# Last pass of a graph network kernel: the rows of 104 of its 416 tiles fetched by one-hot matmuls, the other 312 gathered into places of their own

## The reference, cut to what matters

```
# L3: x_i = x[row], x_j = x[col]; row and col are the edges' two ends
m   = [x_i, x_j - x_i] @ W.T, batch norm, silu        # per edge
out = segment_sum(m, row)                              # one sum per node, added to x
```

## Time and profile before

| | |
|---|---|
| median of 3 runs | 4434.35 us (4432.85 to 4438.28) |
| the profiled execution's own time | 4435.5 us |
| its span | 4433.7 us |
| granted clock of TensorE, mean | 0.892 of 2.4 GHz |
| PE busy | 3310.6 us (75%) |
| DVE busy | 2910.4 us (66%) |
| POOL busy | 3018.6 us (68%) |
| the last pass, from its first gather to the end of the span | 3891.8 to 4433.7 us |

### The profile page before, as it was taken

One profiled execution on the slowest core, in us unless ns is written; L12 is line 12 of the kernel. 1 busy time (PEld: TensorE's weight loads), 2 busy tenths in 40 slices (PEclk: granted clock), 3 DMA queues, 4 the chain that ended last, 5 costly groups with the idle time before them and its releaser, 6 DMA issues.

```text
span 4433.7 us, 80945 instructions
## 1 busy us (share of the span) xinstructions
PE 3310.6 (75%) x20757; PEld 2267.7 (51%) x20758; DVE 2910.4 (66%) x10438; ACT 847.9 (19%) x2207; POOL 3018.6 (68%) x3059
## 2 busy tenths in 40 slices
PE   1269408888887999999687876888858877566666
PEld 1269304554553444443466665666646666445554
DVE  6987319999993111111788887888878888765554
ACT  0000002222221000000122222222212222121121
POOL 2677767788778888840377774777747777467776
PEclk9999999999997999999899996999979999755555
DMA  4310013333458999999222223222232222211112
GB/s 143 108 46 10 17 59 81 88 90 90 92 88 314 356 363 356 363 357 361 80 62 62 61 62 51 63 62 62 62 52 63 62 62 62 33 32 28 28 28 30
DMA packets 295276, 497.76 MB, mean 112 GB/s; under 512 B 165611, under 2 KB 210540, under 8 KB 293674
## 3 DMA queue, kind: packets, MB, share of 16 engines
q1 hardware_dynamic: 120119, 340.02, 21.7%
q0 software_dynamic: 92160, 115.39, 13.6%
q10 hardware_dynamic: 82800, 40.01, 3.1%
HBM read 435.66 MB, written 59.08 MB: 112 GB/s over the span
## 4 chain that ended last, share of the span: by engine, by line
PE 29%; POOL 24%; issue 18%; DMA 16%; DVE 9%; DVEq 1%; SPq 1%; ACT 1%; POOLq 0%; ACTq 0%
PE ps L1565 27%; POOL arena L825 17%; DMA arena<-table,arena 13%; POOL rows_dst L808 7%; DMA rows_dst<-stage,arena 2%; PE ps L1754 1%; DMA arena<-in_edge_attr_dram 1%; DVE arena L1174 1%; DVE arena L1173 1%; DVE arena L1156 1%; DVEq L553 1%; DVE arena L1158 1%; DVE arena L1192 1%; DVE arena L1150 1%; DMA arena<-dense 1%
## 5 line engine op out<-in xcount | busy, mean ns | idle before, releaser
L825 POOL DMA_INDIRECT arena<-table,arena x2080 | 2110.2, 1015 | 1046.5 <-issue 541.3
L1565 PE MATMUL ps<-arena 125*128 (+5 forms) x9976 | 1629.7, 339 | 580.5 <-DVE arena L1192 250.9
L1565 PEld LDWEIGHTS ps<-arena 125*128 125x128 bf16 (+5 forms) x9976 | 1187.8, 206 | 990.8 <-issue 606.5
L1565 PE MATMUL ps<-arena,nodes 125*64 125x500 f32 (+2 forms) x3144 | 651.4, 537 | 34.6 <-DMA arena<-dense 24.1
L1174 DVE TENSOR_SCALAR arena<-iota_row_b,arena 128x128 f32<-128x128 bf16 x2080 | 584.9, 299 | 0.0
L808 POOL DMA_INDIRECT rows_dst<-stage,arena x400 | 401.0, 1002 | 233.0 <-issue 122.2
L779 POOL DMA_INDIRECT rows_src<-stage,stage_at x400 | 479.0, 1197 | 116.4 <-issue 108.4
L1186 DVE TENSOR_TENSOR arena<-ps,arena 128x256 f32<-128x256 f32 x416 | 176.6, 425 | 523.9 <-DMA arena<-table,arena 510.4
L1173 DVE TENSOR_SCALAR arena<-iota_row_b,arena 128x128 bf16<-128x128 bf16 x1664 | 458.4, 277 | 2.7 <-DVE arena L1325 1.1
L1274 DVE TENSOR_TENSOR nodes<-nodes,ps 125x256 f32 (+1 forms) x70 | 27.5, 393 | 609.4 <-PE ps L1754 609.4
L1565 PEld LDWEIGHTS ps<-arena,nodes 125*64 125x64 f32 (+1 forms) x3144 | 244.5, 137 | 351.7 <-issue 320.1
(11 more groups left out here) (286 smaller groups left out, 3510.3 us busy)
## 6 DMA issues: line engine op xcount, KB each, us to landing
arena<-dense SPq DMA_DIRECT2D x240, 750.0 KB, 7.5
nodes<-dense SPq DMA_DIRECT2D x60, 750.0 KB, 8.2
dense<-arena ACTq DMA_DIRECT2D x150, 250.0 KB
arena<-table,arena POOLq DMA_INDIRECT x2080
arena<-dense SPq DMA_DIRECT2D x60, 500.0 KB
arena<-rows_dst SPq DMA_DIRECT2D x208, 96.0 KB
arena<-dense SPq DMA_DIRECT2D x6, 2000.0 KB, 21.5
arena<-pair_rows SPq DMA_DIRECT2D x12, 976.6 KB
```

The source lines that it names most:

```text
L825: nc.gpsimd.indirect_dma_start(rows[:, u, k, 0:width], None, frm, bass.IndirectOffsetOnAxis(ap=p[:, c, j, c_other:c_other + 1].bitcast(I32 ...
L1565: return nc.tensor.matmul(to, lhsT, rhs, start=start, stop=stop, skip_group_check=True)
```

## The change

Only the last pass's way to its rows is replaced; three things are prepared for it earlier. In the changed kernel:

1. With tables (`pair_...`): for each of the 25 blocks of other nodes and each block of own nodes it is known which tiles hold such edges (edges of one own block are sorted by the other's block). Going through the tiles in order, a step is one (tile, block of the other nodes) pair that occurs: at most 104 + 600 = 704 steps for the first 104 tiles. The tables are worked out behind those of before, ahead of `blk_ready`: some 60 DVE instructions, four transposes, a 25-wide product, 20 matmuls of 1 x 384, 30 of 128 x 2, one more, and 15 small DMAs in three round trips to DRAM.
2. In the second of the third layer's passes SP loads all 416 tiles' (key, other) into `src_rows` (852 KB), DVE makes a code for each edge (6 more instructions and a copy), PE turns codes and keys in 8 transposes ahead of its pass, ACT copies them, SP writes them to DRAM. In the third POOL issues 6 indirect DMAs more, DVE one subtraction, and SP writes `turn_rows`.
3. In the last pass SP loads keys, broadcast to all partitions, 256 KB for two units (`load_keys`). DVE makes the turned one-hots directly, 128 x 512 f32 from f16 keys (`turn_step`), with no transpose by PE and no copy by ACT. PE first goes through the 704 steps in 44 iterations of 16: each step is one f32 matmul, turned one-hot (128 columns) by a block's rows in SBUF (64 wide), added to the tile's place in one of four PSUM banks; for each four steps it reads four places and four blocks into registers. ACT moves each 8 finished tiles to `store` and clears the bank. Then come 104 units: four f32 matmuls of the own rows, 64 wide, and as before four f32 matmuls for the sums. POOL meanwhile gathers the rows of the other 312 tiles into `store`, each to a place of its own, in straight code with no ring and no wait for `pay2`.

The arithmetic of the last pass is in f32 where it had been in three bf16 parts. `pay2`, the ring, the bf16 one-hots, their transposes and copies and the split of `t2` are gone from the last pass.

```diff
+PT = 104
+PS = PT + HI * (HI - 1)
+PG, PB, PB0, BURST = 8, 4, 4, 16
+PE_, PU, PR, PK = PS // K, T // K, 4, 6
...
# SP, ahead of blk_ready
+            sp.wait_ge(pair_made, 1)
+            for x in range(3):
+                sp.dma_start(pairs_of[x, 1:HI * HI + 1].rearrange("(s d) -> s d", s=HI), pair_vals[:, x, :]).then_inc(pairs_out, 16)
+                sp.dma_start(pairs_of[x:x + 1, 0:1], zero).then_inc(pairs_out, 16)
+            sp.wait_ge(pairs_out, 16 * 6)
...
+            sp.wait_ge(tables_made, 1)
+            sp.dma_start(pair_tables[0:1], off_i[:, 0:PS]).then_inc(tables_out, 16)
...
+            sp.wait_ge(tables_out, 16 * 4)
             for h in range(2):
                 sp.wait_ge(scattered[h], 16 * SG * G2)
# SP, last pass
+            def load_keys(q):
+                if q >= PK // 2:
+                    sp.wait_ge(turned_made, 2 * (q - PK // 2) + 2)
+                at_ = 2 * q % PK
+                sp.dma_start(keys3[:, at_:at_ + 2, :].rearrange("p e c -> p (e c)"),
+                             turn_rows[2 * K * q:2 * K * (q + 1), :].rearrange("r e -> (r e)").partition_broadcast(128)).then_inc(
+                                 keys_in[q % (PK // 2)], 16)
# POOL, last pass
-            gather(EP_L3, pay2, C2_OTHER, table, D)
+            pool.wait_ge(turn_out, 16 * 2)
+            hold(pool, table_in, 32 * (NQ * EP_L3 + 1))
+            for n in range((T - PT) // K):
+                for k in range(K):
+                    if n and k == 2:
+                        hold(pool, gathered[(n - 1) % U], 16 * K * (EP_L3 * NB + (n - 1) // U + 1))
+                    t = PT + n * K + k
+                    nc.gpsimd.indirect_dma_start(
+                        store[:, t, :], None, table,
+                        bass.IndirectOffsetOnAxis(ap=src_rows[:, t, C2_OTHER:C2_OTHER + 1].bitcast(I32), axis=0)).then_inc(gathered[n % U], 16)
# DVE, last pass
+            def turn_step(e):
+                if e % 2 == 0:
+                    v.wait_ge(keys_in[e // 2 % (PK // 2)], 16 * (e // PK + 1))
+                if PR <= e < PE_ + PR:
+                    v.wait_ge(turned_used, e - PR + 1)
+                elif e >= PR:
+                    v.wait_ge(local_added, e - PR - PE_ + 1)
+                nc.vector.tensor_scalar(ohT3[:, e % PR, :], keys3[:, e % PK, :], iota_p[:, 0:1], None, ALU.is_equal).then_inc(turned_made, 1)
+            def hots(u):
+                if u >= PR:
+                    v.wait_ge(hots_used, u - PR + 1)
+                for k in range(K):
+                    ins = nc.vector.tensor_scalar(oh3[:, u % PR, k, :], iota_row_b[:], src_rows[:, u * K + k, C2_KEY:C2_KEY + 1], None, ALU.is_equal)
+                ins.then_inc(hots_made, 1)
+            for e in range(PE_ + 1):
+                turn_step(e)
+            hots(0)
+            for u in range(PU):
+                if u + 1 < PU:
+                    turn_step(PE_ + u + 1)
+                    hots(u + 1)
...
+                v.wait_ge(local_added, u + 1)
+                nc.vector.tensor_tensor(s3[:, u % PR], store[:, u * K:(u + 1) * K, :], lin3(u), ALU.add).then_inc(sums_made, 1)
# PE, last pass
+            with pe.Fori(0, PS // BURST) as i:
+                need3 = load_values(pe, pair_need[0:1, bass.ds(i, 1)], 1, PT // PG + 1)[0]
+                pe.reg_alu(at_least_one, need3, 1, ALU.max)
+                hold(pe, pair_bank_free, at_least_one)
+                for e in range(BURST // K):
+                    offs = load4(pair_off[0:1, bass.ds(i * BURST + e * K, K)], PB0 * 512, 8 * 512 - D)
+                    blks = load4(pair_blk[0:1, bass.ds(i * BURST + e * K, K)], 0, (HI - 1) * D)
+                    pe.wait_ge(turned_made, i * (BURST // K) + (e + 1))
+                    for k in range(K):
+                        ins = mm(flat[:, bass.ds(offs[k], D)], ohT3[0:LO, e % PR, k * 128:(k + 1) * 128],
+                                 gathered_table[:, bass.ds(blks[k], D)], start=False, stop=False)
+                    ins.then_inc(turned_used, 1)
+            pe.wait_ge(pair_bank_free, PB + PT // PG)
...
             def turn3(i, u, before, more):
+                offs = load_unit(tab_at, 0, i, u, (HI - 1) * D)
+                pe.wait_ge(turned_made, i * U + (PE_ + u + 1))
                 if before == 2:
+                    pe.wait_ge(sums_made, i * U + (u - 1))
+                for k in range(K):
+                    ins = mm(lin3(u)[:, k, :], ohT3[0:LO, (PE_ + u) % PR, k * 128:(k + 1) * 128], local_table[:, bass.ds(offs[k], D)], start=k == 0)
+                ins.then_inc(local_added, 1)
+                if before == 2:
+                    sum_up3(i, u - 2)
# ACT, last pass
+            for g in range(PT // PG):
+                end = load_counts(a, pair_end[0:1, g:g + 1], 1, PE_)[0]
+                hold(a, turned_used, end)
+                bank = PB0 + g % PB
+                nc.scalar.copy(store[:, g * PG:(g + 1) * PG, :].rearrange("p t d -> p (t d)"), ps[:, bank, :]).then_inc(rows_kept, 1)
+                a.wait_ge(rows_kept, g + 1)
+                nc.scalar.copy(ps[:, bank, :], zeros[:]).then_inc(pair_bank_free, 1)
```

More of the change, by code:

```diff
@@ new lines, in _ @@
+            v.sem_inc(pair_made, 1)
+            v.wait_ge(pairs_in, 16 * 5)
+            link(nc.vector.tensor_tensor(pair_col[:, 1:3, :], pair_col[:, 1:3, :], pair_col[:, 3:5, :], ALU.subtract))
+            link(nc.vector.tensor_scalar(pair_mid, pair_col[:, 0, :], float(-PH), None, ALU.add))
+            for h in range(5):
+                for half, first in enumerate((pair_col[:, 0, :], pair_mid)):
+                    ins = nc.vector.tensor_scalar(pair_begun[:, h, half * PH:(half + 1) * PH], iota_t[0:LO, 0:PH], first[:, h:h + 1],
+                                                  None, ALU.is_ge)
@@ new lines, in _ @@
+            ins.then_inc(pair_ready, 1)
+            v.wait_ge(pair_done, 3)
+            for half in range(2):
+                nc.vector.scalar_tensor_tensor(tile_row[:, half * PH:(half + 1) * PH], iota_t[0:1, 0:PH], float(half * PH),
+                                               ps[0:1, half, 0:PH], ALU.add, ALU.add)
+            for c in range(PC):
+                nc.vector.tensor_scalar(tile_col[:, c:c + 1], ps[:, 4, 2 * c:2 * c + 1], iota_p[:, 0:1], float(128 * c), ALU.add, ALU.add)
+            nc.vector.tensor_scalar(blk_i.rearrange("p (b t) -> p b t", b=2), ps[0:1, 2:4, 0:PH], float(D), None, ALU.mult)
@@ L1622, in _ @@
             ins.then_inc(starts_summed, 1)
+            pe.wait_ge(pair_ready, 1)
+            for x, frm in enumerate((col_sums[0:HI, 1, :], col_sums[0:HI, 0, :], start_of[0:HI, :], tiles[0:HI, :])):
+                ins = nc.tensor.transpose(ps[0:HI, 4, x * HI:(x + 1) * HI], frm, ident[0:HI, 0:HI])
+            ins.then_inc(pair_done, 1)
+            pe.wait_ge(pair_ready, 2)
+            mm(ps[0:HI, 7, 0:1], d_before[:, 0:HI], pair_incl[:, HI - 1:HI]).then_inc(pair_done, 1)
+            pe.wait_ge(pair_ready, 3)
+            for x in range(2):
+                for half in range(2):
+                    for h in range(5):
+                        mm(ps[0:1, 2 * x + half, 0:PH], pair_col[:, 1 + x, h:h + 1], pair_begun[:, h, half * PH:(half + 1) * PH],
+                           start=h == 0, stop=h == 4)
+            for c in range(PC):
+                for h in range(5):
+                    ins = mm(ps[:, 4, 2 * c:2 * c + 2], pair_begun[:, h, c * 128:(c + 1) * 128], pair_col[:, 1:3, h], start=h == 0, stop=h == 4)
+            ins.then_inc(pair_done, 1)
+            pe.wait_ge(pair_ready, 4)
+            mm(ps[0:1, 5, 0:PT // PG], one_each[:, 0:1], n_before).then_inc(pair_done, 1)
             pe.wait_ge(blk_ready, 1)
@@ L1825, in _ @@
                 hold(pe, local_ready, l + 1)
+                if l == 1:
+                    pe.wait_ge(codes_ready, 1)
+                    for x, frm in enumerate((code, own_key)):
+                        for c in range(4):
+                            ins = nc.tensor.transpose(ps[0:T // 4, 4 + x, c * 128:(c + 1) * 128], frm[:, c * (T // 4):(c + 1) * (T // 4)], ident[:])
+                    ins.then_inc(codes_turned, 1)
+                    pe.wait_ge(codes_copied, 1)
                 def turn2(i, u, before, more):
@@ new lines, in _ @@
+            for g in range(PB):
+                ins = mm(ps[:, PB0 + g, :], zeros_b[:, 0:128], zeros_b[:], stop=False)
+            ins.then_inc(pair_bank_free, PB)
+            gathered_table = nodes[0:LO, 3, :]
+            local_table = nodes[0:LO, 4, :]
+            with pe.Fori(0, PS // BURST) as i:
[10 more added lines that the diff above has]
+                    ins.then_inc(turned_used, 1)
```

256 lines of the change are left out of this document (212 added, 44 removed).

## The result

The changed kernel took **4612.65 us** (median of 4 runs, 4608.09 to 4614.78); the kernel before, run beside it, 4436.32 (4432.85 to 4442.82). The ratio is 1.0394, 95% interval 1.0376 to 1.0412: slower by 3.9%, 176 us, where I had forecast 47 and a range that ended at 4600. The direction held, the size did not. The profiled execution took 4610.87 us with a span of 4609.1.

A forecast was written before the change was run, and what follows sets the result against it. PE's instruction queue was to bound the last pass: start 3890 + 330 + 1.5 + 244.4 = 4466, with the tail 4479, plus 3 for tables a span of 4482, execution 4484, so 4483 us. The range was 4452 to 4600.

The forecast's parts named there:

- What is prepared earlier: Tables ahead of pass 0: a 72.5 us chain against 69 us of cover, +3 us, from nothing to +12.
- The first half: Last pass, 704 steps in 44 iterations: PE's queue needs 7.5 us an iteration, 330 us.
- in the bound above, not in the sum: First half: each matmul's second address register was counted in the forecast's bounds, 7.2 to 8.0 us an iteration, not in 7.5.
- The second half: Last pass, 104 units: PE's queue needs 2.35 us a unit at the full clock, 244 us.
- rival 1: Second half at half clock: the array bounds at 3.56 us a unit, 4609 at most, 4595 if groups run together; chance 0.18.
- the short loop: The first half as forecast, 7.5 us an iteration and 330 us, which the half-clock rival's total also used.
- rival 2: Last pass: PE's queue runs ahead, loads hide behind the array, POOL's last gather decides; 4306 us, chance 0.10.
- Rivals 3 and 4: Last pass: POOL bounds at over 1.85 us a gather, 4490 and more, 0.04; register loads dragged out by traffic, 4646, 0.02.

The follow-up runs named there:

- all_gathered: Changed kernel without the 704 one-hot steps and their copies out of the banks; POOL gathers all 416 tiles' rows: 4446.87 us.
- short: Changed kernel with the loop of steps cut to 17 iterations in place of 44: 4400.74 us, 0.9914 of the kernel before.
- no_loads: Changed kernel without the two register loads ahead of every four steps, which use constant addresses (wrong rows for 104 tiles): 4343.60 us.
- first_full: border_keep plus sixteen wide matmuls of zeros ahead of the loop of steps and two behind every four steps: 4515.78 us.
- load_eight: Changed kernel with the bank offsets of eight steps read by one register load in place of two: 4597.39 us.
- border_keep: border_burst plus one wide matmul of zeros behind every unit's sums: 4508.34 us.
- border_burst: Changed kernel with sixteen 128x512 bf16 matmuls of zeros between the two halves: 4607.15 us.
- short_burst: Changed kernel with both edits, 17 iterations (short) and sixteen wide matmuls between the halves (border_burst): 4380.00 us, 4334.06 to 4391.35 in 6 runs.
- wide_both: Changed kernel with one 128x512 bf16 matmul of zeros behind every four steps and behind every unit's sums: 4665.41 us.
- The best kernel of the study: Changed kernel with 17 iterations, sixteen wide matmuls of zeros between the halves and one behind every unit's sums: 4329.11 us, 0.9756 of the kernel before.

## Why the prediction was right and wrong

**The bound before, and the start.** Right. The pass was POOL's, and all_gathered, which keeps POOL's 416 gathers, is back at the time of before. What is prepared earlier was put at 3 us, and the first node-row transposes of the last pass do start at 3878.75 us in place of 3875.71. That is luck. The 3 us came from the tables, a chain of 72.5 us that was to outlast its cover of 69. In the changed kernel SP issues the last DMA of the tables at 619.90 us and the loads of pass 0 at 637.78, where before they were issued at 641.38:

```profile
619.90 0.25 SPq L799 DMA_DIRECT2D pair_counts<-arena  x1
637.78 1.86 SPq L807 DMA_DIRECT2D arena<-rows_dst  x4
```

So the tables took under 50 us and cost nothing there, and in this pair of traces pass 0 began 4 us earlier, not up to 12 later. In other traces with the same code up to there the last pass starts later still, at 3879.6 (short) to 3890.7 (no_loads), so one pair of traces does not price the preparation; all_gathered, 5 us over before, is the nearest to a price.

**The first half.** Right in mechanism, 7% short. "The queue bounds this half at either clock" is what first_full and load_eight show. An iteration is 8.01 us where the sum gave 7.5: 0.5 x 44 = 22 us. The mis-sized term is the four matmuls whose two addresses each come from registers, 0.60 us of queue where I took the 0.50 of four with one address; I had left the second register "in the bound above, not in the sum", and it belonged in the sum. With two loads at 0.50 and the wait, four steps are 1.70 and not 1.6; the rest is 0.1 more an iteration around the branch.

**The second half.** Here the prediction failed: "I take the full clock." A unit took 3.38 us at half clock, not 2.35, and 103 x 1.03 = 106 of the 127 us are that. It is rival 1, which I had given 0.18. Its 4595 to 4609 lies 4 to 18 us below the 4612.65, and part of that nearness is luck: it took 3.56 us a unit, 18 us too many in all, and the short loop, 22 too few. Units of 3.5 us at 0.50 of the clock were also what I had named as a sign of being wrong. The pace for the full clock was right: 2.28 us in border_keep, with one more matmul in each unit, and 18.7 / 8 = 2.34 in no_loads. What was wrong is the reason. I argued that PE "would be busy all the time", and from 2740 to 2760 us, where a busy PE had got its full clock. In the changed kernel PE was busy 330.00 of 330 us at 0.50. Those earlier 20 us are a pass with other matmuls, most of them 128 columns wide; I compared busy shares and not what the array was busy with. That the shapes are the cause is likely and not shown: no run changed the shapes alone. The Trainium skill, TensorE: Matmul & The Clock Gate, section Why this matters for your kernels, advises to keep TensorE busy continuously to get its full clock. By that rule the second half would have had it, as I forecast; the row disagrees, and the row decides. What does lift it, the runs show: wide matmuls back to back (border_burst). Narrow ones then can hold it, for 37 us there, 150 in short_burst, and in no_loads until PE waited for a gather 386 us on; with a wide one behind each unit's sums they held it in all 104 units (border_keep).

**The link between the two that I missed.** I treated the clock of each half by itself. no_loads shows one chain: a loop whose queue keeps up holds the full clock that the clearing of the banks gave it, and hands it on. The loop cost 22 us more than forecast, and the half behind it 106. The second does not hang on the first: load_eight's loop ran at the 7.5 us of the forecast and left half clock all the same, so the forecast's own loop would most likely have done so too. no_loads took away loads and address arithmetic together; at what pace between 3.6 and 7.5 us the full clock is kept, no run shows.

**The loop's length.** I took the 704 steps as work and never asked how many of them this graph uses. 65 of 176 groups of four do, and ACT's copies, which wait for exactly these counts, would have told. It does not touch the forecast, since all 704 run. But it is the largest thing in the pass, 217 us.

**POOL.** Forecast: last gather near 4284 and far off the path. Measured 4308.8, at 1.335 us each in place of 1.2595, and off the path. 44 gathers waited for a landing while the key loads took the DMA to 91 GB/s. In no_loads, at 170 GB/s, the last came at 4326.2, and DVE waited for gathers near the end: PE's queue did run ahead there, as in rival 2, and the whole ended at 4343.6 and not at the 4306 of rival 2, because its gathers came later. Rivals 3 and 4 did not happen: the loads took 332 ns, as before the change.

## What to carry to other kernels

A pass may be limited by one engine's queue and pay for it elsewhere: here an array fed slowly dropped to half clock, and the narrow matmuls that followed were busy without a gap and stayed there. So ask of each stage at which clock it *begins*, and compare the shapes of its matmuls too, and not its busy share alone, with a stage that had the full clock; sixteen wide matmuls on zeros at the border, and one in each unit, were worth 108 us here. And where a loop is sized for the worst case, read from what waits on its counts how much of it the data at hand uses, before anything in it is tuned.

## What the runs showed of the hardware

- PE busy 330 of 330 us with 64- and 96-column f32 matmuls stayed at 1.2 GHz; sixteen 128x512 bf16 matmuls of zeros, 6.2 us, brought the next ones to 2.4 (border_burst). One such matmul a unit kept the full clock where it was there (border_keep) and did not bring it where it was not (wide_both). What exactly decides there stays open.
- Units at the full clock without that extra matmul are on an edge: the clock fell behind a gap of 0.5 us at the loop's branch after 37 us in border_burst and after 150 in short_burst, stayed through ten such gaps in no_loads, and six runs of one kernel spread over 57 us. Once it had fallen it did not come back in the 300 us that were left.
- A register load takes 301 ns for one value, 332 for four (medians; single ones up to 531 in the changed kernel's loop) and 588 for eight. The Trainium skill, DMA: Bandwidth & Descriptors, section Latency and other measured facts, has a floor of about 600 ns for it; the medians for one and four values lie well below it.
- The best kernel of the study, at 4329 us, depends on the shorter loop. One that reads its number of iterations from the counts on PE, DVE and SP was not tried.
